# One-core adapter kernel: the head rebuilt (bias loads at once, GpSimd makes the picking matrix and a third of W_down's high halves, SP alone fetches activations and W_up)

## What is computed

```python
x: (64, 64, 512)   W_down: (3, 512, 256)   W_up: (3, 256, 512)   # float32
h = gelu(x[b] @ W_down[e] + b_down[e], approximate=False)         # e = itok[b]
h = x[b] + h @ W_up[e] + b_up[e]
out[b] = (h - mean(h)) * rsqrt(var(h) + 1e-5) * ln_w[e] + ln_b[e]
```

## Time and profile before

| | us |
|---|---|
| median of 3 runs | 142.29 (142.18 to 142.58) |
| profiled execution, device time | 142.74 |
| its span in the profile | 140.9 |
| PE busy | 126.1 (89% of the span) |
| DVE busy | 113.2 (80%) |
| POOL busy | 100.8 (72%) |
| ACT busy | 86.5 (61%) |

### The profile page before, as it was taken

How to read it: one execution, slowest core, us unless ns; L and a number is a source line. 1 busy time by engine, 2 the same in 40 slices (tenths; PEclk the granted TensorE clock), 3 DMA queues, 4 the chain that set the end, 5 groups by cost and what they waited for, 6 DMA issues and landing times.

```text
span 140.9 us, 4062 instructions
## 1 busy us (share of the span) xinstructions
PE 126.1 (89%) x840; PEld 113.3 (80%) x841; DVE 113.2 (80%) x274; ACT 86.5 (61%) x179; POOL 100.8 (72%) x109
## 2 busy tenths in 40 slices
PE   6739873999999999999999999999999999999820
PEld 6539662999999989998999999999999999998610
DVE  2749679588888888888888888888988888897981
ACT  1659774456666666666666666666666666666500
POOL 3000484056888988888889888888888888889760
PEclk9999999999999999999999999999999999999998
DMA  1939999844223455455454555544456633332464
GB/s 36 364 100 363 278 338 331 247 124 142 73 85 126 100 179 149 148 151 157 154 133 166 169 135 146 169 151 151 153 155 152 149 74 74 79 74 49 99 170 133
DMA packets 13200, 21.94 MB, mean 156 GB/s; under 512 B 2297, under 2 KB 3842, under 8 KB 13186
## 3 DMA queue, kind: packets, MB, share of 16 engines
q1 hardware_dynamic: 8146, 14.43, 36.0%
q10 hardware_dynamic: 5040, 7.36, 17.1%
HBM read 13.39 MB, written 8.65 MB: 156 GB/s over the span
## 4 chain that ended last, share of the span: by engine, by line
PE 76%; DMA 7%; DVE 5%; issue 2%; DVEq 2%; SPq 2%; POOL 2%; ACT 1%; POOLq 1%; ACTq 0%
PE hg_ps L766 31%; PE y_ps L791 30%; PE xT_ps L752 10%; DMA x_sb<-in_x_dram 5%; PE hg_ps L775 5%; POOL res L351 2%; DMA itok_all_i<-in_itok_B_dram 2%; DVE wu_lo L246 1%; SPq L274 1%; DVEq L585 1%; DVEq L61 1%; DVE hb L604 1%; SPq L264 1%; DVE r_stats L616 0%; ACT normed L431 0%
## 5 line engine op out<-in xcount | busy, mean ns | idle before, releaser
L336 POOL TENSOR_TENSOR xb<-x_sb,bu_rows 128x512 f32<-128x512 f32 x33 | 43.8, 1329 | 14.7 <-ACT bu_rows L453 13.2
L351 POOL TENSOR_TENSOR res<-normed,lnb_rows 128x512 f32<-128x512 f32 x31 | 40.0, 1291 | 14.3 <-ACT normed L431 14.3
L411 ACT ACTIVATE g<-hb 128x256 f32<-128x256 f32 x33 | 13.9, 420 | 38.0 <-DVE hb L604 38.0
L616 DVE BATCH_NORM_STATS2 r_stats<-y_ps 128x6 f32<-128x512 f32 x33 | 23.0, 696 | 8.7 <-issue 8.0
L637 DVE SCALAR_TENSOR_TENSOR scaled<-y_ps,r_mv,lnw_rows 128x512 f32<-128x512 f32 x33 | 24.5, 744 | 0.1
L596 DVE TENSOR_TENSOR xT_lo<-xT_ps,xT_hi 128x512 fp32r<-128x512 f32 x33 | 22.8, 690 | 2.2 <-ACT xT_hi L406 2.2
L791 PE MATMUL y_ps<-wu_hi,gT_hi 128*128 x66 | 23.5, 437 | 0.7 <-ACT gT_hi L416 0.7
L766 PE MATMUL hg_ps<-wd_hi,xT_hi 128*128 x132 | 23.7, 302 | 0.3 <-ACT xT_hi L406 0.3
L342 POOL TENSOR_TENSOR rstd<-var_eps,half_neg 128x1 f32<-128x1 f32 x33 | 18.2, 552 | 6.2 <-DVE var_eps L625 6.2
L791 PE MATMUL y_ps<-wu_lo,gT_hi 128*128 x66 | 20.7, 394 | 2.1 <-DVE wu_lo L246 2.1
L431 ACT ACTIVATE normed<-scaled,rstd 128x512 f32<-128x512 f32 x31 | 22.4, 723 | 0.0
(11 more groups left out here) (81 smaller groups left out, 151.3 us busy)
## 6 DMA issues: line engine op xcount, KB each, us to landing
x_sb<-in_x_dram SPq DMA_DIRECT2D x66, 128.0 KB, 3.0
...
wd<-in_L_cond_W_down_dram ACTq DMA_DIRECT2D x3, 512.0 KB, 4.4
wu<-in_L_cond_W_up_dram ACTq DMA_DIRECT2D x3, 512.0 KB, 6.2
...
```

Of the source, the lines that this page charges most:

```text
L336: pool.tensor_tensor(xb[:, c % DEEP, :], x_sb[:, c % FAR, :], bu_rows[:, ds(e * H, H)], ALU.add).then_inc(xb_ready, 1)
L351: pool.tensor_tensor(res[:, c % FAR, :], normed[:, c % PAR, :], lnb_rows[:, ds(e * H, H)], ALU.add).then_inc(res_ready, 1)
L616: dve.bn_stats(r_stats[:, c % DEEP, :], y_ps[c % YBANKS][:]).then_inc(stats_ready, 1)
```

## The change

- **Biases.** SP no longer waits for `itok` before it asks for them.
- **GpSimd** makes `pick` in place of ACT, and the high half of W_down's third expert.
- **ACT** casts W_down's first expert before the biases. It asks for no W_up. The copies of the down biases out of PSUM go to DVE, and PE spreads the up biases first.
- **SP** fetches W_up as well, by "slots": slot 0 holds the expert of the first tile, so a small DVE operation writes the numbers of the experts into free entries of `io_table`. SP's new order is x0, x1, W_up slot 0, x2, slot 1, `lnw_rows`, x3, slot 2, `lnb_rows`, x4 and so on. Four entries of the table are read at once.
- **W_up's high and low halves** are made one slot at a time, between the bodies of tiles 0 to 2, and `up` of tiles 0, 1 and 2 each waits for one more of them.
- **DVE** builds the store addresses (`slot_store`) after the body of tile 2, not in the head.
- **PE** transposes x1 before `down(0)` and runs `down(1)` before `transpose_g(0)`.

The diff, cut to its core (semaphores and helper arguments that only follow from it are left out):

```diff
-    WARM_UPS = 8, 2, 2, 2
+    WARM_UPS = 9, 3, 2
...
+        def load_w_up(eng, slot, e):
+            eng.dma_start(wu[:, slot, :, :], w_up[ds(e, 1), :, :].rearrange("a (c p) n -> p (a c) n", p=P)).then_inc(
+                wu_in[slot], 16)
+        def w_down_high(eng, e):
+            copy = eng.copy if eng is nc.scalar else eng.tensor_copy
+            eng.wait_ge(wd_in[e], 16)
+            return copy(wd_hi[:, e * KH * BN:(e + 1) * KH * BN], wd[:, e, :, :].rearrange("p c n -> p (c n)"))
...
         def _(sp):
             sp.wait_ge(biases_clear, 1)
-            sp.wait_ge(itok_in, 16)
             sp.dma_start(biases[0:E, :], b_down).then_inc(biases_in, 16)
             sp.dma_start(biases[E:B_ROWS, :], b_up.rearrange("e (a n) -> (e a) n", n=BN)).then_inc(biases_in, 16)
-            sp.wait_ge(slots_ready, 1)
...
-            for t in range(4):
-                load(t, t, entries(t, 0, 2))
+            head_regs = [sp.alloc_register(f"head{i}") for i in range(4)]
+            sp.wait_ge(slots_ready, 1)
+            sp.reg_load(head_regs, io_table[0:1, 0:4])
+            load(0, 0, [sp.snap(reg, min_val=0, max_val=B - 1) for reg in head_regs[0:2]])
+            load_half(sp, 1, 0, sp.snap(head_regs[3], min_val=0, max_val=B - 1))
+            sp.reg_load(head_regs[:1], io_table[0:1, 4:5])
+            load_half(sp, 1, 1, sp.snap(head_regs[0], min_val=0, max_val=B - 1))
+            sp.wait_ge(slots_ready, 2)
+            sp.reg_load(head_regs, io_table[0:1, 5:9])
+            load_w_up(sp, 0, sp.snap(head_regs[0], min_val=0, max_val=E - 1))
+            load(2, 2, [sp.snap(reg, min_val=0, max_val=B - 1) for reg in head_regs[1:3]])
+            load_w_up(sp, 1, sp.snap(head_regs[3], min_val=0, max_val=E - 2) + 1)
             sp.dma_start(lnw_rows[:], rows_of(ln_w, P)).then_inc(lnw_in, 16)
+            sp.reg_load(head_regs[:3], io_table[0:1, 9:12])
+            load(3, 3, [sp.snap(reg, min_val=0, max_val=B - 1) for reg in head_regs[:2]])
+            load_w_up(sp, 2, sp.snap(head_regs[2], min_val=0, max_val=E - 3) + 2)
+            sp.dma_start(lnb_rows[:], rows_of(ln_b, P)).then_inc(lnb_in, 16)
             load(4, 4, entries(4, 0, 2))
-            sp.dma_start(lnb_rows[:], rows_of(ln_b, P)).then_inc(lnb_in, 16)
             for t in range(5, STORE_A_LAG):
                 load(t, t, entries(t, 0, 2))
...
+            pool.iota(top_row[:], pattern=[[-1, E]], base=E - 1, channel_multiplier=0).then_inc(const_ready, 1)
...
+            pool.wait_ge(const_ready, 6)
+            pool.tensor_copy(pick[:], ident[:, 0:B_ROWS].unsqueeze(2).broadcast_to([P, B_ROWS, P])).then_inc(
+                pick_ready, 1)
+            w_down_high(pool, E - 1).then_inc(wd_hi_last, 1)
...
-            act.wait_ge(const_ready, 5)
-            act.copy(pick[:], ident[:, 0:B_ROWS].unsqueeze(2).broadcast_to([P, B_ROWS, P])).then_inc(pick_ready, 1)
+            w_down_high(act, 0).then_inc(wd_hi_ready, 1)
             act.wait_ge(biases_in, 32)
             act.copy(biases_hi[:], biases[:]).then_inc(biases_hi_ready, 1)
-            wd_high(0)
-            wd_high(1)
-            for e in range(E):
-                load_w_up(act, e)
-            wd_high(2)
-            for part in range(len(bd_banks)):
-                keep_down_bias(part)
+            w_down_high(act, 1).then_inc(wd_hi_ready, 1)
             for e in range(E):
                 keep_up_bias(e)
             x_hi(0, 0)
+            x_hi(1, 1)
...
-            wu_high(1)
-            x_hi(1, 1)
             gelu(0, 0)
-            wu_high(2)
             g_hi(0, 0)
             seed(0, 0)
             x_hi(2, 2)
+            wu_high(1)
             def body(t, c):
...
+            body(1, 1)
+            wu_high(2)
+            for t in range(2, STORE_B_LAG):
+                body(t, t)
...
+            first_expert = tile_expert[:, 0:1].broadcast_to([1, E])
             link(dve.tensor_scalar(tile_expert[:], key_filled[:, 1:1 + SLOTS:2], B.bit_length() - 1, RANGE // B - 1,
                                    ALU.logical_shift_right, ALU.bitwise_and))
+            dve.tensor_tensor(io_view[:, 1:1 + E, 2], first_expert, top_row[:], ALU.min)
             pair_view = up_down[:].rearrange("p (t n) -> p t n", n=2)
-            dve.tensor_copy(pair_view[:, :, 0], tile_expert[:])
+            dve.tensor_tensor(pair_view[:, :, 0], tile_expert[:], tile_expert[:, 0:1].broadcast_to([1, TILES]),
+                              ALU.subtract)
             dve.tensor_copy(pair_view[:, 0:TILES - 1, 1], tile_expert[:, 1:TILES]).then_inc(slots_ready, 1)
             dve.wait_ge(biases_hi_ready, 1)
...
+            for e in range(E - 1):
+                dve.wait_ge(wd_hi_ready, e + 1)
                 w_down_low(dve, e).then_inc(wd_lo_ready, 1)
+            for part in range(len(bd_banks)):
+                keep_down_bias(part)
+            dve.wait_ge(wd_hi_last, 1)
+            w_down_low(dve, E - 1).then_inc(wd_lo_ready, 1)
...
-            wu_low(0)
+            x_lo(1, 1)
             dve.wait_ge(bd_ready, len(bd_banks))
             down_bias(0, 0)
-            x_lo(1, 1)
-            wu_low(1)
+            wu_low(0)
             g_lo(0, 0)
-            wu_low(2)
             down_bias(1, 1)
             x_lo(2, 2)
+            wu_low(1)
             def body(t, c):
...
+            body(1, 1)
+            wu_low(2)
+            body(2, 2)
+            dve.tensor_copy(key_f[:], key_filled[:])
+            link(dve.tensor_scalar(slot_batch[:], key_filled[:, 1:1 + SLOTS], B - 1, None, ALU.bitwise_and))
+            link(dve.tensor_copy(slot_batch_f[:], slot_batch[:]))
+            link(dve.tensor_tensor(slot_same[:], key_f[:, 1:1 + SLOTS], key_f[:, 0:SLOTS], ALU.is_equal))
+            link(dve.scalar_tensor_tensor(out=slot_store[:], in0=slot_same[:], scalar=float(B), in1=slot_batch_f[:],
+                                     op0=ALU.mult, op1=ALU.add))
+            dve.tensor_copy(io_view[:, STORE_A_LAG:, 2], slot_store[:, 0:SLOTS:2]).then_inc(slots_ready, 1)
+            for t in range(3, 6):
                 body(t, t % UNROLL)
...
-            spread_row(bd_banks[1], 0, 2).then_inc(spread, 1)
             for e in range(E):
                 spread_row(y_ps[e], 0, E + 2 * e)
-                spread_row(y_ps[e], 1, E + 2 * e + 1).then_inc(spread, 1)
+                spread_row(y_ps[e], 1, E + 2 * e + 1).then_inc(up_spread, 1)
+            spread_row(bd_banks[0], 0, 0)
+            spread_row(bd_banks[0], 1, 1).then_inc(down_spread, 1)
+            spread_row(bd_banks[1], 0, 2).then_inc(down_spread, 1)
...
             transpose_x(0, 0)
-            warm_up(WARM_UPS[3], hg_ps[1])
-            pe.wait_ge(w_hi_ready, E)
+            transpose_x(1, 1)
+            pe.wait_ge(wd_hi_ready, E - 1)
+            pe.wait_ge(wd_hi_last, 1)
             pe.wait_ge(bd_ready, len(bd_banks))
             down(0, 0, expert_of(pe, 0))
-            transpose_x(1, 1)
             e0, e1 = experts_from(0)
+            down(1, 1, e1)
             transpose_g(0, 0)
-            down(1, 1, e1)
             transpose_x(2, 2)
```

66 lines of the change are left out of this document (32 added, 34 removed).

## The result

The changed kernel takes 148.58 us (median of 4 runs, 147.62 to 148.83) against 142.39 us for the kernel before beside it (142.18 to 142.58): a ratio of 1.042, 95% interval 1.037 to 1.047. It is 4% slower; 141.7 us was predicted. Its profiled execution took 148.41 us, 5.67 more than that of before. A median is over all runs of a kernel, a ratio only over those within about 1.5% of its fastest one, so the two do not always agree. Medians of the changed kernel's variants are compared with 148.58 us across chips and rest on few runs each, so differences of 1 to 2 us between them are shown only where the trace shows them too.

A forecast was written before the change was run, and what follows sets the result against it. The head was taken to bound the kernel: PE enters its steady period when x4 lands. From 142.29 us, 1.1 us gained by x4 and 0.5 us lost to DVE gave 141.7 us, range 140.0 to 143.1 us (8 in 10).

The forecast's parts named there:

- what bounds the kernel: Head: when PE enters its steady 3.49 us period counts; a shift of `transpose_g(2)` shifts the total unless DVE falls behind.
- The bias part: Head: biases asked for at once let PE's bias pass begin and end about 2 us earlier, worth nothing alone.
- compute: PE's head work is ready long before x4, with `up(0)` ending at about 20 to 21 us.
- rival 1: GpSimd's `pick` holds the sort 1.9 us, so all fetches follow and the total is 143.6 us; chance 0.09.
- SP's queue: SP's requests in the head: x0's first half goes out at 7.95 us, W_up slot 0 at 12.0 us.
- When x4 lands: Head: 12.0 + 11.0 (3.93 MB at 356 GB/s) + 3.0 gives 26.0 us (24.5 to 27.4); 1.1 us gained.
- the time beyond the bytes: Input loads: what passes between issue and landing besides the bytes, taken as 3.0 us between 1.5 and 4.4 us.
- The clock: PE in the head: fewer warm-up matmuls cost nothing that is waited for, as the granted clock reads 1.00.
- DVE's new debt: DVE between bodies: `wu_low(2)` and the store addresses (1.22 us) make PE late; 0.5 us lost, bounds nothing and 1.3 us.
- Rival 2: x4 at 27.4 us or 1.3 us of DVE debt: 142.6 or 142.5 us, a little of both 143.0; chance 0.26.

The follow-up runs named there:

- e8: The kernel before with one part of the change alone, the biases asked for at once and not after `itok`: 143.65 us (ratio 1.005).
- e2: The changed kernel with `lnb_rows` asked for behind x4, as before the change: 144.80 us (ratio 1.012).
- e3: The changed kernel with the store addresses back in DVE's head and `lnb_rows` asked for behind x4: 142.72 us (ratio 0.9995).
- e14: The changed kernel with `lnb_rows` asked for by ACT, on another queue, instead of SP: 151.23 us.
- e10: The changed kernel with W_up asked for by ACT again instead of SP: 147.79 us (ratio 1.033).
- e7b: The changed kernel with dummy matmuls on a free bank where PE waits, 7 ahead of x3 and 15 ahead of x4: 147.33 us (ratio 1.029).

## Why the prediction was wrong

The account of what bounds the kernel held: what the head does to `transpose_g(2)` it does to the total, and what DVE loses behind it stays lost. x4 was the gate. Three sizes were wrong, all the same way.

**The bias part and compute** were as said, but for the price of the first in e8. `pick` took 1.14 us on GpSimd, not the 1.7 us of the estimate, and was over at 3.14 us; `own_only` stood at 3.59 us, so rival 1 did not happen. `biases_lo` started at 6.92 us, the bias pass at 7.48 us, x1 was transposed at 12.24 us, `up(0)` ended at 19.7 us. That the biases at once are worth nothing alone was too kind: e8 shows that in the kernel before, where ACT asks for W_up, they pull W_up ahead of x0.

**SP's queue**: right within 0.7 us. x0's first half went out at 7.29 us and slot 0 at 11.33 us (12.0 predicted), since the first read of four took 0.51 us, where 1.07 us was assumed; the second took 0.88 us, as assumed.

**When x4 lands** is the step that failed: 26.0 us by the sum, 24.5 to 27.4 in its bounds, 28.45 us measured. The 3.93 MB were counted right and went out sooner than assumed. Up to the last megabyte the sum also held: x3's second half landed at 21.4 us (21.6 predicted) and W_up slot 2 at 22.8 us (23.1). What is left, `lnb_rows` and x4, is 1.05 MB, 2.9 us in the sum, and took 5.7 us. The sum treated the queue as one line in which only the bytes ahead count, at 356 GB/s to the end, and both are wrong here:

- The rate. The stretch 24.0 to 28.5 us carried 213 GB/s, and 12.0 to 28.5 us 287 GB/s (307 in the kernel before). With 287 GB/s, 3.0 us beyond the bytes and slot 0 at 11.33 us the sum gives 28.0 us for x4, but then 22.6 us for x3, which is too late; so a lower rate throughout is not the explanation. The bounds came from the time beyond the bytes alone, though the earlier trace rows had 275 to 404 GB/s; with 275 GB/s the prediction's own sum gives 29.3 us.
- The line. Transfers of SP's queue did not land in the order asked for: x5's first half, asked for 1.2 us behind x4's second, landed at 26.2 us, 2.2 us ahead of it, so bytes asked for later took part of the rate. The sum had `lnb_rows` as 786 kB, 2.2 us at 356 GB/s; by e2 it costs x4 2.55 us (25.9 against 28.45), near that. By e3 and e14 the second half that stands behind it is late wherever that is (x5's at 30.1 us, x3's at 25.8 us and not 21.4).

Even without `lnb_rows` ahead, x4 lands at 25.9 us in e2 and 24.7 us in e3, where the sum would have 23.8. The late requests for W_up are a part of this, as e10 shows; how much of it, no run separates.

**The clock** was put at "no cost", since it read 1.00 in the stretches shown and PE had idled before. The waits for x3 and x4 (1.81 and 3.19 us) follow from the forecast itself, and after PE had stood from 19.7 to 21.5 us the granted clock fell to 0.50. It cost 1.0 us up to the mark (2.88 less 1.89 us) and 0.54 in the next period, and 1.25 us of the total by e7b. With x4 2.45 us late, the 1.0 us, and 0.3 us for starting again after a wait (the chain has 0.66 us for transposing x4 and 0.04 us ahead of it, where it has 0.44 us without a wait), the mark is at 31.58 us in the chain and not at 27.8.

**DVE's new debt** was put at 0.5 us, bounds 0 and 1.3 us; PE stood 1.65 us for it, and `transpose_g(4)` lost 2.18 us. The addresses were priced by their rows in an idle head, 1.22 us, although the same text says that a GpSimd instruction costs DVE up to its own length; this was used for the 1024-column subtractions and for the sort, and not for six operations on one partition. Two of them paid it, 1.13 and 1.04 us, just the 2.15 us by which the chain is longer. The lower bound had a fault of its own: "x4 later than 26.5 us hides it". x4 was later, and this hid `wu_low(2)`, after which DVE stood idle for 2.74 us until `up(1)` was done. It could not hide the addresses, which stand behind tile 1's statistics and so start only after that wait.

Rival 2 (x4 late or the debt in full) was the right one in kind, and its price, 142.5 to 143.0 us, took one of the two at a time and the clock for free.

Still open: why the second half of a tile (partitions 64 to 127) lands 2.4 to 3.3 us behind the first for x4, x5 and x6, when it is asked for 0.67 us later, and what makes one DVE operation stand beside GpSimd and another not (below). No run separated these. The first is not always so: in e10 the halves of x4, x5 and x6 landed 0.7 to 0.9 us apart.
